# A graph and expert network on one core: the order of the expert stage's rows and the place of its weight folding are changed

## The reference, cut to what matters

```
x = x + L0_gnn(layernorm(x), adj)      # attention-like mix by adj
x = x + L0_ffn(layernorm(x))           # 30 iterations: tanh, silu, layernorm, 128x128 product
x = x + L1_gnn(layernorm(x), adj)      # relu(features W1 + adj features W2 + bias)
x = x + L1_ffn(layernorm(x))           # 8 experts, each token uses its best 2
# L1_ffn, per token t with best experts a, b of softmax(x Wr + br):
#   xn = normalize(x[t]);  y_e = gelu((xn*g_e + b_e) W1_e + b1_e) W2_e + b2_e
#   out[t] = w_a*y_a + w_b*y_b          (W1_e 128x512, W2_e 512x128)
```

## Time and profile before

| what | value |
|---|---|
| median of 3 runs | 2807.94 us (2805.99 to 2810.53) |
| the profiled execution | 2804.9 us, its span 2803.1 us |
| granted TensorE clock, mean | 0.97 |
| busy: PE, DVE, ACT, POOL | 89%, 74%, 65%, 72% |
| first normalize of the experts to the span's end | 1986.7 to 2803.1 us |

### The profile page before, as it was taken

How to read it: one execution, slowest core, us unless ns; L and a number is a source line. 1 busy time by engine, 2 the same in 40 slices (tenths; PEclk the granted TensorE clock), 3 DMA queues, 4 the chain that set the end, 5 groups by cost and what they waited for, 6 DMA issues and landing times.

```text
span 2803.1 us, 62675 instructions
## 1 busy us (share of the span) xinstructions
PE 2489.5 (89%) x19950; PEld 2340.0 (83%) x19951; DVE 2075.3 (74%) x5754; ACT 1809.0 (65%) x2185; POOL 2029.8 (72%) x1592
## 2 busy tenths in 40 slices
PE   6839999999999999999999999886588888888887
PEld 5839999999999999999999999882577777777777
DVE  6999999999999999999999998674122222222222
ACT  3779999999999999999999973220222222222222
POOL 5779999999999999999999997775232332323323
PEclk9969999999999999999999999995799999999999
DMA  9000000000000000000000000411433333333332
GB/s 267 35 1 1 0 0 0 0 0 0 0 0 0 0 0 0 0 0 0 0 0 0 0 1 32 132 43 49 141 129 125 123 125 125 127 123 126 123 123 76
DMA packets 123642, 141.98 MB, mean 51 GB/s; under 512 B 14951, under 2 KB 76547, under 8 KB 123553
## 3 DMA queue, kind: packets, MB, share of 16 engines
q1 hardware_dynamic: 112450, 122.86, 13.3%
q0 software_dynamic: 9088, 17.14, 1.9%
q10 hardware_dynamic: 2016, 0.95, 0.1%
HBM read 36.35 MB, written 24.58 MB: 22 GB/s over the span
## 4 chain that ended last, share of the span: by engine, by line
DVE 54%; PE 29%; issue 9%; ACT 4%; another core or an unknown queue 2%; SPq 1%; DMA 0%; DVEq 0%; POOL 0%; POOLq 0%; ACTq 0%
DVE pair_stats L639 23%; DVE state L682 17%; PE psum L1244 12%; PE psum L1235 10%; DVE state L661 6%; PE psum L1072 3%; ACT adjT L1022 3%; PE psum L1062 2%; DVE it_vars L643 1%; DVE x_stats L639 1%; DVE resid L709 1%; DVE state L678 1%; DVE resid L669 0%; PE psum L1208 0%
## 5 line engine op out<-in xcount | busy, mean ns | idle before, releaser
L1072 PEld LDWEIGHTS psum<-w_ffn,turned 128*128 128x128 f32 x7680 | 1010.0, 192 | 36.1
L1072 PE MATMUL psum<-w_ffn,turned 128*128 128x128 f32 x7680 | 1013.6, 275 | 0.0
L495 POOL TENSOR_TENSOR it_rstd<-it_vars,minus_half 128x8 f32<-128x8 f32 x480 | 786.3, 1638 | 0.0
L498 POOL TENSOR_TENSOR state<-state,it_rstd 128x768 f32<-128x768 f32 x480 | 708.8, 1477 | 37.7
L639 DVE BATCH_NORM_STATS2 pair_stats<-state 128x6 f32<-128x256 f32 x1920 | 684.9, 417 | 0.0
L1062 PE MATMUL psum<-ident,state 128*128 128x128 f32 x4352 | 596.7, 281 | 72.3 <-DVE state L678 43.0
L574 POOL DMA_INDIRECT out_dram<-resid,adjT x156 | 161.3, 1034 | 554.5 <-DVE resid L909 544.1
L682 DVE SCALAR_TENSOR_TENSOR state<-state,psum 128x1024 f32<-128x1024 f32 x464 | 560.7, 1208 | 1.3 <-ACT state L943 0.7
L1022 ACT ACTIVATE adjT<-psum 128x512 f32<-128x512 f32 x312 | 186.4, 597 | 578.5 <-PE psum L1235 578.4
L1062 PEld LDWEIGHTS psum<-ident,state 128*128 128x128 f32 x4352 | 478.2, 143 | 90.8 <-issue 69.5
L936 ACT COPY turned<-psum 128x1024 f32<-128x1024 f32 x480 | 485.9, 1012 | 78.5 <-PE psum L1062 41.9
(11 more groups left out here) (192 smaller groups left out, 1710.0 us busy)
## 6 DMA issues: line engine op xcount, KB each, us to landing
adjT<-resid SPq DMA_DIRECT2D x312, 256.0 KB, 2.3
adjT<-sorted_rows SPq DMA_DIRECT2D x156, 66.5 KB
resid<-in_x_dram SPq DMA_DIRECT2D x16, 512.0 KB, 7.3
state<-in_adj_dram SPq DMA_DIRECT2D x16, 512.0 KB, 7.3
adjT_dram<-adjT SPq DMA_DIRECT2D x7, 512.0 KB, 3.7
adjT<-adjT_dram SPq DMA_DIRECT2D x7, 512.0 KB, 3.5
out_dram<-resid,adjT POOLq DMA_INDIRECT x156, 2.5
sorted_rows<-state,slot POOLq DMA_INDIRECT x128
```

The lines of the kernel that those rows point to most:

```text
L495: nc.gpsimd.tensor_tensor(it_rstd[s % 8][:, :], it_vars[s % 4][:, :], minus_half[:, 0:TILES], ALU.pow).then_inc(it_pow, 1)
L498: nc.gpsimd.tensor_tensor(values[s][:, 0:POOL_TILES, :], values[s][:, 0:POOL_TILES, :], wide(it_rstd[s % 8][:, 0:POOL_TILES]), ALU.mult).t ...
L1072: last = nc.tensor.matmul(dst[:, t, :], stationary(t), moving(t), start=bias is None and m == 0, stop=m == len(terms) - 1, skip_group_chec ...
```

## The change

It has two parts. In the experts, DVE does `normalize(o + 3)` ahead of `finish(o - 1)`; PE loads the numbers of both experts of a slab ahead of its first product, and does `second_product` ahead of `turn`. Before the experts, the foldings use four PSUM banks and are spread (PE: two pairs of sums in slots 18 and 19, one in 20 and 21, two behind the tables; DVE: two slots later, the last four around the tables), the last slot is dropped, the copy of token numbers moves to POOL's earlier loop, the fillings start from `ends_ready` (when the regions' ends are known) with 10 on SP and 19 on the ACT queue, and SP issues four matrices, then rows, then four more between rows.

```diff
-        psW = [psum[:, 2 + j, :] for j in range(2)]
+        psW = [psum[:, 2 + j, :] for j in range(4)]
...
-        GNN1_SLOTS = STREAMS + PLACE_LAG + 1
+        GNN1_SLOTS = STREAMS + PLACE_LAG
...
-        FOLD_FROM = STREAMS + X3_LAG
+        FOLDS = {18: (0, 1), 19: (2, 3), 20: (4,), 21: (5,)}
+        LATE_FOLDS = (6, 7)
...
+            sp.wait_ge(ends_ready, 1)
+            for c in range(SP_FILLS):
+                fill(sp, c)
             sp.wait_ge(tables_ready, 1)
-            for c in range(0, PAIRS + 1, 2):
-                fill(sp, c)
             sp.wait_ge(w1_folded, NE)
-            for u in range(8):
+            for u in range(4):
                 load_weights(u)
...
             for n in range(4 + AHEAD):
                 load_rows(n)
+                if n in (2, 3):
+                    load_weights(2 * n)
+                    load_weights(2 * n + 1)
...
+                nc.gpsimd.tensor_copy(state[s][:, :, TOKEN].bitcast(I32), ids[:, s * TILES:(s + 1) * TILES])
...
-                    nc.gpsimd.tensor_copy(state[s][:, :, TOKEN].bitcast(I32), ids[:, s * TILES:(s + 1) * TILES])
...
+            def fold_weights(e):
+                dve.wait_ge(fold_psum, e + 1)
+                nc.vector.scalar_tensor_tensor(w1_all[:, e, :], w1_all[:, e, :], params[:, e, 0:1], psW[e % 4],
+                                               ALU.mult, ALU.add).then_inc(w1_folded, 1)
...
+                for e in FOLDS.get(k - 2, ()) if k < GNN1_SLOTS - 1 else ():
+                    fold_weights(e)
...
-            nc.vector.tensor_copy(pad_row[:, :], pair_end[:, :])
+            nc.vector.tensor_copy(pad_row[:, :], pair_end[:, :]).then_inc(ends_ready, 1)
...
+            fold_weights(4)
+            fold_weights(5)
             dve.wait_ge(table_psum, 1)
...
+            for e in LATE_FOLDS:
+                fold_weights(e)
             dve.wait_ge(tables_ready, 1)
...
                 for o in range(EACH):
+                    if not end or o < EACH - 3:
+                        normalize(i, o + 3)
                     if not first or o >= 1:
                         finish(i, o - 1, not first or o >= 5)
-                    if not end or o < EACH - 3:
-                        normalize(i, o + 3)
...
-            act.wait_ge(tables_ready, 1)
-            for c in range(1, PAIRS + 1, 2):
+            act.wait_ge(ends_ready, 1)
+            for c in range(SP_FILLS, PAIRS + 1):
                 fill(act, c)
...
                 for o in range(2 * EACH):
+                    if o % 2 == 0 and (not first or o >= 2):
+
+                        whose = [expert_of(i, o - 2), expert_of(i, o - 1)]
                     first_product(i, o)
+                    if not first or o >= 2:
+                        second_product(i, o - 2, whose[o % 2])
                     if o % 2 == 0 and (not end or o < 2 * EACH - 4):
                         turn(i, o // 2 + 2)
-                    if not first or o >= 2:
-                        second_product(i, o - 2, expert_of(i, o - 2))
```

More of the change, by code:

```diff
@@ L196, in network @@
         w2_all = over_resid(4, 4).rearrange("p (e c d) -> p e c d", e=NE, c=HC)
-        b2_all = over_resid(8, 1).rearrange("p (e d) -> p e d", e=NE)
-        b1_row = over_resid(9, 4).rearrange("p (e h) -> p e h", e=NE)[0:1]
-        fold_wide = over_resid(13, 1).rearrange("p (e d) -> p e d", e=NE)
+        b2_all = over_resid(13, 1).rearrange("p (e d) -> p e d", e=NE)
+        b1_row = over_resid(8, 4).rearrange("p (e h) -> p e h", e=NE)[0:1]
+        fold_wide = over_resid(12, 1).rearrange("p (e d) -> p e d", e=NE)
         y_out = [over_resid(14, 1)[:, D * q:D * (q + 1)] for q in range(4)]
@@ L280, in network @@
         pair_tables = sem("pair_tables")
+        ends_ready = sem("ends_ready")
         centred_logits = sem("centred_logits")
@@ L376, in fill @@
             queue.dma_start(dst, pad[:, :].bitcast(F32)).then_inc(pads_in, 16)
+        SP_FILLS = 10
         @block.sync
@@ L405, in _ @@
                 sp.dma_start(w2_all[:, e], E_W2[e].rearrange("(c p) d -> p c d", p=P)).then_inc(experts_in[1], 16)
-            sp.wait_ge(x3_ready, 9)
+            sp.wait_ge(x3_ready, 12)
+            sp.dma_start(b1_row, E_b1.unsqueeze(0)).then_inc(experts_in[3], 16)
+            sp.wait_ge(x3_ready, 14)
             sp.dma_start(b2_all, E_b2.partition_broadcast(P)).then_inc(experts_in[2], 16)
-            sp.wait_ge(x3_ready, 13)
-            sp.dma_start(b1_row, E_b1.unsqueeze(0)).then_inc(experts_in[3], 16)
             def load_rows(n):
@@ L825, in _ @@
                     route(a)
-                if k == FOLD_FROM - 1:
-                    dve.wait_ge(x3_ready, 14)
+                if k == STREAMS:
                     nc.vector.tensor_scalar(fold_wide, fold[:, :].unsqueeze(2).to_broadcast([P, NE, D]), 1.0 / D, None,
                                             ALU.mult).then_inc(fold_ready, 1)
[L830 to L834, removed]
+                for e in FOLDS.get(k - 2, ()) if k < GNN1_SLOTS - 1 else ():
+                    fold_weights(e)
             table_at = [0]
@@ L1134, in _, with fold_sums @@
             iteration(STEPS, tail=True)
+            def fold_sums(e):
+                if e == 0:
+                    pe.wait_ge(fold_ready, 1)
+                    pe.wait_ge(experts_in[0], 16)
+                    pe.wait_ge(experts_in[3], 16)
+                    pe.wait_ge(q_copied, STREAMS)
+                elif e == 2:
+                    pe.wait_ge(x3_ready, STREAMS)
+                elif e >= 4:
+                    pe.wait_ge(w1_folded, e - 3)
+                nc.tensor.matmul(psW[e % 4], fold_wide[:, e, :], w1_all[:, e, :], start=True, stop=False,
+                                 skip_group_check=True)
+                nc.tensor.matmul(psW[e % 4], frac[0:1, :], b1_row[:, e, :], start=False, stop=True,
+                                 skip_group_check=True).then_inc(fold_psum, 1)
             for k in range(GNN1_SLOTS):
@@ L1195, in _ @@
                     last.then_inc(logit_psum, 1)
[L1196 to L1209, removed]
+                for e in FOLDS.get(k, ()):
+                    fold_sums(e)
             pe.wait_ge(diag_ready, 1)
```

## The result

The changed kernel takes 2850.07 us (median, 2847.17 to 2852.02 in 4 runs) beside 2806.97 us for the kernel before on the same chip: ratio 1.0156, 95% interval 1.0134 to 1.0177. That is 43 us slower, more than twice the 20 that were forecast; the time lies inside the stated range (2800 to 2860).

The account below looks back on a forecast made before the run. A ring of waits, no full engine, was taken to set the expert slab's 5.22 us. +42 + 4 + 3 - 29 = +20 us on 2804.9 gives 2825, and the median 3.0 above: 2828 us, range 2800 to 2860.

Parts of the forecast that it names:

- The ring: Expert stage: normalize, two additions behind register loads, sum, store, scale, next normalize; 5.54 us per looped slab against 5.22.
- the start's -29 us: Before the experts: fillings, weights and scatter side by side all end near 1955.6, first rows about 28 us earlier; -21 to -37.
- The ring's signs: Expert loop: normalize idles some 2.5 us for L578, slab 5.5 us, PE waits at second product, busy below 80%.
- +42 and +3 in the loop: Expert loop: +0.32 us in each of 132 slabs gives +42; POOL's occasional late store, no longer hidden, gives +3.
- the first load's link: Expert loop: normalize to first bias addition, over a register load: 0.96 us, from 0.77 written out plus 0.19.
- The late store: POOL's store starts a few us late in two of the 132 slabs, hidden before but not in a ring: +3 us.
- +4 for the written-out slabs: About 20 expert slabs outside the loop: 5.16 us each against 4.96, together +4 us.
- PE's pairs against the 11.4 us wait: Start: PE's four early pairs (16 us) may delay the count, losing up to 8 us; without the wait, 6 to 8 earlier.
- DVE's sequencer does not run past a held normalize: Denies a rival: register load done during normalize's wait, ring 4.85 us, time 2727; chance 0.10 with other shorter rings.
- PE's two loads are covered: Expert stage: loads fit the ring's spare 1.8 us; rival, not covered: PE needs 5.8 us, time 2868, chance 0.06.
- the other case, some +250: Rival in the expert loop: PE drops to 1.2 GHz, four products over 7 us per slab, some +250 us; chance 0.02.
- the load's price: Register load in the ring: 305 ns by the trace, taken; by the skill's 600 ns, ring 6.1 us, some 79 us more.

Follow-up runs that it names:

- e2: Only DVE's expert order changed (normalize ahead of finish), in the kernel before: 2879.07 us, 1.0255 of the kernel before.
- e4: The changed kernel with POOL computing scale one slab earlier, scale(n + 5) instead of scale(n + 4): 2569.62 us, 0.9155 of the kernel before.
- e5: The changed kernel with DVE's two register loads of a finish moved ahead of the normalize, POOL's order untouched: 2630.58 us, 0.9366 of the kernel before.
- e1: The changed kernel without its expert part, DVE's and PE's expert orders as before: 2791.66 us, 0.9935 of the kernel before.
- e7: The kernel of e4 with both queues waiting for the whole scatter ahead of the fillings: 2583.12 us, 0.9189 of the kernel before.
- e9: The kernel of e4 with four pairs of sums right behind the last count, four behind the tables: 2539.35 us, 0.9142 of the kernel before.
- e6: The kernel of e4 with all sums and foldings moved behind the tables: 2572.13 us, 0.9148 of the kernel before.
- e13: The kernel of e4 measured once more, beside e14 on one chip: 2575.02 us, 0.9154 of the kernel before.
- e14: The kernel of e9 measured once more, beside e13 on one chip: 2573.81 us, 0.9141 of the kernel before.

## Why the prediction was right and wrong

The ring was right in mechanism and nearly in size; the step that failed is the start's -29 us, of which 13 to 18 came. The ring's signs came as named: the normalize idles 2.51 us in nearly every slab, released by L578, the slab is 5.6 us, PE waits at its second product, and its busy share is 75%. "The first rows are loaded near 1955" did not come: they were at 1969.8.

- *A new ring through DVE and POOL, closed by the normalize's place ahead of the finish.* Right, and shown four ways: every normalize waits for L578, DVE's edit alone closes the ring (e2), it opens with one number on POOL (e4), and it shrinks by the two loads when these are taken out of it (e5). Its forecast length, 5.54, was 0.08 short.
- *+42 and +3 in the loop*: measured +50.4. What was mis-sized is the first load's link (1.04, not 0.96, some 10 us in 132 slabs; in nine of the eleven rounds of the loop one slab has both load links near 1.2 and takes 6.0 us, which I had not foreseen). The end of the scale to the normalize was 0.04, not 0.07, which gave 4 us back. The late store was there: one slab of 8.22 us and one of 6.02, together 3.1 more than the usual 5.57, as forecast.
- *+4 for the written-out slabs*: measured +8.3, because the links with loads are 0.93 and 0.84 in the last eleven slabs and 1.01 and 0.79 in slabs 4 to 11, not 0.77 each. I had taken both from one place where the load stood behind a sum.
- *-29 at the start (-21 to -37)*: this failed. Measured -14.2 in the profiled executions, -13 over nine traces and -18 (-12 to -25) by e1's times. Two steps of it: "from about 1933 on" the last slots came 3.6 us later, and "19 on the ACT queue take 19 to 20 us" took 30, so the fillings ended at 1967.6 and not 1954. I priced them by a stretch of the kernel before in which nothing ran beside them (1.0 us each), and moved them beside the scatter. I had taken them as limited by their queue only. e7 shows 19.0 us for them alone. By an estimate, the slow fillings cost 11 us of the missing 15: in e9, where only the scatter was left to wait for, the rows followed its last issue by 2.1 us, which here would be 1958.7 instead of 1969.8. The other 3 us (1958.7 against 1955.6) are the later slots and scatter. The fillings' length is shown; what lengthens them is not.
- *PE's pairs against the 11.4 us wait*: still open. With no sums ahead of the counts the slots came 14 us earlier than in e4 once (e6) and 4 us later than in e13 the other time (e14).
- *The rivals.* DVE's sequencer does not run past a held normalize: the links are 1.04 and 0.97 with the loads behind it and 0.26 and 0.27 with them ahead of it (e5), and in the kernel after the load starts only when the normalize does. The Trainium skill ("TensorE: Matmul & The Clock Gate", section "Architectural detail") gives VectorE a queue eight deep and calls it strictly first in, first out. I had weighed the depth alone, as room for an early load; the traces agree with the order: only loads ahead of the wait ran during it. PE's two loads are covered (e4's PE is 99% busy). PE stayed at 2.4 GHz in nearly all of the loop (0.99). My price for the other case, some +250, was too low by its own numbers: four products of 1.91 make 7.64 us per slab, (7.64 - 5.22) x 132 = +320. The upper edge of the range, by its own terms, comes to 2864 and not 2860. Of the load's price: its own row is 318 ns in the median in the kernel after, about half of the 600 ns floor of the Trainium skill ("DMA: Bandwidth & Descriptors", "Latency and other measured facts"). With the address work around it a load costs the ring 0.70 to 0.78.

The start, the loop and the written-out slabs were off by 15, 5 and 4 us in the profiled executions, all the same way, so 20 became 45 there and 43 in the medians. That the time still lies inside the range owes to the range's width: the start's -14 is outside its own -21 to -37.

**Still open:** what the unnamed waits beside the scatter are. Shown is that they and the slow fillings come and go together, and that neither the mean DMA share nor the chip decides it. An experiment on the scatter itself was not made.

## What to carry to other kernels

Before an instruction is moved ahead of another, follow what it waits for through the other engines' written orders: here the producer's order on POOL had to move with it by one, and that alone turned +1.6% into -8.5%. On DVE, put register loads ahead of a wait, not behind it: in e5 they ran while the engine was held. Price a moved DMA by a stretch in which its new neighbours run; the old place is no evidence.

## What was unexpected of the hardware

- A register load with its address work cost 0.70 to 0.78 us of a ring, of which the load's own row is about 0.32; moved ahead of a wait of 2.5 us it cost the ring nothing (e5: links of 0.26 and 0.27).
- The kernel before took 2804.85 us in one set of runs and 2777.81 in another on the same chip, and the same code, e9 and e14, had its first normalize at 1942.4 and at 1980.2. Unnamed waits on DVE (up to 10.4 us in the kernel after) and a slowing of fillings from 1.0 to 1.6 us each were both absent in the faster set, at a higher DMA share.
- PE's granted clock fell below 1.00 in eleven of fifteen windows of 50 us in e2's loop, down to 0.89, but in the kernel after in two of fifteen (0.97 and 0.93), though PE's busy share is 75% in both loops. What sets them apart was not looked into.
